# Second expert loop of a four-layer kernel: batch 0's rows gathered from slot 27 on, tile stores shared out anew, one register load per slot

## The chip, the cores and the metric

The kernel is one program on one core of a Trainium2 chip. The metric is the device time of one execution in microseconds (us); lower is better.

## The reference, cut to what matters

Four batches of 512 tokens with 128 features pass through four pairs of a cross-attention and a feed-forward block, all in fp32. Two of the feed-forward blocks are mixtures of experts:

```python
# L0: 8 experts, each token goes to one;  L1: 16 experts, each token goes to its three best
x = x + L0_ffn(layernorm(x))      # top_idx = argmax(gate_logits); y = relu(x @ w1[e] + b1[e]) @ w2[e] + b2[e]
x = x + L1_xattn(layernorm(x), ctx)
raw_gate = softmax(x_ @ gate); _, topk_idx = top_k(raw_gate, 3)
x = x + sum over e of gate_topk[..., e] * (relu(x_ @ W1[e] + b1[e]) @ W2[e] + b2[e])    # L1_ffn
x = x + L2_xattn(layernorm(x), ctx)
...
```

## The kernel before, in words

The program's steps are numbered 0 to 7 (attention 0, experts 1, attention 2, experts 3, attention 4, feed-forward 5, attention 6, feed-forward 7). Steps 1 and 3 are **expert loops**. Each engine has its own instruction stream, written out by hand and joined to the others by semaphores, so the order of the code is the order of the work.

**Routing.** For each batch VectorE finds every token's experts and its rank among the tokens of that expert (`route`). GpSimd then writes the normalised rows to their places in `rowbuf` in DRAM by indirect DMAs (`scatter`, 12 for a batch in step 3, two in flight). Every expert has a region there, so its tokens stand in order of batch, and a tile is 128 rows of one region.

**Slots.** The loop goes through the tiles in slots: 23 in step 1, 63 in step 3. In a slot SyncE (SP) loads the tile `xs` from `rowbuf` (`tile_load`), TensorE transposes it (`turn`), multiplies it by the expert's first weights one slot later (`hidden`) and by its second ones two slots later (`second`); ScalarE takes the transposed tile out and applies the bias and the relu. VectorE copies the first weights of a slot four ahead of their use and adds the last bias four slots later (`add_bias`), which writes the tile `ys`. There are 8 places for `xs` and 8 for `ys`. A tile `ys` is stored in `outbuf` by SP, 8 slots behind its load, or in step 3 by GpSimd: all odd slots up to 31 (`own_store`, `SHARE`).

**Which tile stands in which slot** is worked out on the chip, by small matmuls on TensorE and short operations on VectorE: `early_list` gives the first tiles (`EARLY`: 4 and 8) as soon as three batches are routed, and `tile_list` the rest once all four are. Each list is read into registers: SP reads a tile's place (`tiles_of`, one register load per slot, 31 slots ahead), TensorE and VectorE read its expert (`known_at`: from slot `FROM` on two numbers per slot, until all are known). After the first 8 slots of step 3, SP writes one tile of zero rows behind each of the 16 regions.

**Gathering.** GpSimd reads the rows of each batch back by indirect DMAs, 4 per batch in step 1 and 12 in step 3 (`gather`, two in flight). Before a batch it waits until the slots that can hold that batch's rows are stored: `PRIOR[l][b]` is their number, and it waits for the last 8 of them. VectorE adds the gathered rows to `x` (`add_experts`): in step 3 batch 0 beside slots 54, 56 and 58, batch 1 beside slots 59 and 61 and after the loop, batches 2 and 3 inside attention 4. GpSimd also works out the root of each batch's variance (`power`), between the gathers.

```python
PRIOR = {1: (15, 19, 19, 23), 3: (35, 47, 51, 63)}
SHARE = 33
```

## Time and profile before

| | us |
|---|---|
| median of 3 runs | 554.27 (553.14 to 560.3) |
| the profiled execution, its own time | 557.48 |
| span from its first to its last instruction | 555.8 |

| engine | busy us | share of the span |
|---|---|---|
| TensorE (PE) | 418.5 | 75% |
| VectorE (DVE) | 333.5 | 60% |
| ScalarE (ACT) | 239.4 | 43% |
| GpSimd (POOL) | 226.9 | 41% |

The rows of the profile come from that one execution, so a stage is read against its 557.48 us, of which 1.7 lie outside the span. No engine is busy all the time: what counts at each place is which wait ends last. In this execution the first expert loop takes the stretch from 77 to 136 us, attention 2 that from 136 to 210, the second loop that from 229 to 342, and attention 4 follows.

### The profile page before, as it was taken

To read this page: it belongs to the slowest core of one execution; us is meant where nothing else is said; L and a number is where in the kernel's file an instruction comes from. 1 tells how busy PE (TensorE), PEld (TensorE's weight loads), DVE (VectorE), ACT (ScalarE), POOL (GpSimd) and SP (SyncE) were. 2 spreads that over 40 slices of the span, in tenths; PEclk is the share of its full clock that TensorE was granted. 3 is DMA by queue.
4 is the path that set the end of the run, shared out by engine and by line. 5 is a ranking of instruction groups with operands and counts; after the bars stand their busy time and mean duration, and the time that the engine had idled before them with its cause. 6 is when DMAs were issued, how large, how long until landed. Compare 5 with 4: busy or idle time off the path is not lost.

```text
span 555.8 us, 10030 instructions
## 1 busy us (share of the span) xinstructions
PE 418.5 (75%) x2604; PEld 347.2 (62%) x2604; DVE 333.5 (60%) x1141; ACT 239.4 (43%) x635; POOL 226.9 (41%) x286
## 2 busy tenths in 40 slices
PE   5788758997889898549899436857799999972550
PEld 4667748897567685338799435536586768761440
DVE  5755535563878765124445317477676577858887
ACT  2333315554444422425677223433555755652321
POOL 3512740016515777641114655663311254543215
PEclk9795559998999857678999778778699999995555
DMA  7899646782191111343335322110000000000002
GB/s 194 269 404 406 158 141 214 274 296 71 36 357 47 49 38 39 110 119 106 95 103 153 94 57 60 37 44 10 0 2 1 1 0 2 1 0 1 1 1 75
DMA packets 63301, 56.50 MB, mean 102 GB/s; under 512 B 12180, under 2 KB 49262, under 8 KB 63118
## 3 DMA queue, kind: packets, MB, share of 16 engines
q1 hardware_dynamic: 56094, 44.98, 25.3%
q0 software_dynamic: 4608, 9.45, 5.8%
q10 hardware_dynamic: 2544, 1.44, 0.9%
q8 instruction: 23, 0.38, 0.3%
q14 instruction: 32, 0.26, 0.2%
HBM read 24.12 MB, written 31.72 MB: 100 GB/s over the span
## 4 chain that ended last, share of the span: by engine, by line
PE 27%; DMA 19%; DVE 17%; SPq 12%; issue 9%; POOL 7%; DVEq 5%; ACT 4%; POOLq 0%; ACTq 0%
SPq L424 12%; DMA rowbuf<-h_sb,slots 7%; PE bank L2236 5%; PE bank L2249 5%; DMA vZ<-outbuf,slots 5%; PE bank L2090 4%; POOL rowbuf L638 3%; PE bank L2106 3%; DMA h_sb<-outbuf,slots 3%; PE bank L2095 2%; PE bank L2228 2%; ACT xn L1625 2%; DVE stats L823 2%; POOL rstd L615 2%; DMA outbuf<-h_sb 1%
## 5 line engine op out<-in xcount | busy, mean ns | idle before, releaser
L2249 PE MATMUL bank<-wall,r 128*128 x436 | 70.3, 296 | 20.1 <-DVE h_sb L1292 19.8
L1719 ACT ACTIVATE r<-bank,b 128x128 f32<-128x128 f32 x218 | 66.1, 366 | 34.1 <-PE bank L2236 33.8
L615 POOL TENSOR_TENSOR rstd<-veps,mhalf 128x4 f32<-128x4 f32 x32 | 33.8, 1057 | 114.0 <-DVE veps L828 113.7
L638 POOL DMA_INDIRECT rowbuf<-h_sb,slots x64 | 62.6, 978 | 34.9 <-DMA rowbuf<-h_sb,slots 14.9
L2249 PEld LDWEIGHTS bank<-wall,r 128*128 128x128 f32 x436 | 60.1, 206 | 22.3 <-issue 21.3
L665 POOL DMA_INDIRECT vZ<-outbuf,slots x40 | 39.1, 978 | 65.0 <-DMA outbuf<-h_sb 46.2
L2236 PE MATMUL bank<-on,e_sb 128*128 128x128 f32 x348 | 58.4, 301 | 0.0
L2106 PEld LDWEIGHTS bank<-vB,eT 128*128 128x128 f32 x384 | 51.7, 209 | 0.0
L2106 PE MATMUL bank<-vB,eT 128*128 128x36 f32 x384 | 51.5, 284 | 0.0
L2236 PEld LDWEIGHTS bank<-on,e_sb 128*128 128x128 f32 x348 | 50.6, 213 | 0.0
L1711 ACT COPY on<-bank 128x128 f32<-128x128 f32 x86 | 23.1, 268 | 63.4 <-PE bank L2228 61.5
L1649 ACT COPY eT<-bank 128x512 f32<-128x512 f32 x48 | 28.1, 585 | 47.1 <-PE bank L2095 47.1
L1292 DVE TENSOR_TENSOR h_sb<-bank,b2all 128x128 f32<-128x128 f32 x86 | 24.7, 289 | 37.6 <-PE bank L2249 37.3
L1298 DVE COPY e_sb<-wall 128x256 f32 (+1 forms) x75 | 25.1, 337 | 31.8 <-PE bank L2236 19.9
L2228 PE MATMUL bank<-ident,h_sb 128*128 128x128 f32 x86 | 26.7, 311 | 22.4 <-DMA h_sb<-rowbuf 15.4
L2095 PEld LDWEIGHTS bank<-ident,e_sb 128*128 128x128 f32 x192 | 25.9, 154 | 23.2 <-issue 10.8
L2090 PE MATMUL bank<-aB,xnT_all 128*128 128x512 f32 x64 | 35.3, 640 | 5.3 <-DVE e_sb L1229 4.6
L2095 PE MATMUL bank<-ident,e_sb 128*128 128x128 f32 x192 | 32.5, 297 | 3.1 <-ACT e_sb L1645 2.0
L2228 PEld LDWEIGHTS bank<-ident,h_sb 128*128 128x128 f32 x86 | 13.1, 153 | 30.3 <-DMA h_sb<-rowbuf 17.7
L823 DVE BATCH_NORM_STATS2 stats<-x 128x6 f32<-128x128 f32 x128 | 27.9, 281 | 2.9
L1225 DVE TENSOR_REDUCE mx<-bank 128x16 f32<-128x512 f32 x32 | 21.9, 684 | 10.8 <-PE bank L2090 10.5
L1625 ACT ACTIVATE xn<-x,nmr,rstd 128x128 f32<-128x128 f32 x48 | 19.7, 483 | 15.7 <-POOL nmr L622 15.7
(303 smaller groups left out, 845.9 us busy)
## 6 DMA issues: line engine op xcount, KB each, us to landing
outbuf<-zero SPq DMA_DIRECT2D x17, 1024.0 KB, 13.6
wall<-in_w SPq DMA_DIRECT2D x4, 2048.0 KB, 13.9
h_sb<-rowbuf SPq DMA_DIRECT2D x86, 64.0 KB, 2.0
outbuf<-h_sb SPq DMA_DIRECT2D x70, 64.0 KB, 1.9
rowbuf<-zero SPq DMA_DIRECT2D x24, 64.0 KB, 1.5
x<-in_x ACTq DMA_DIRECT2D x4, 256.0 KB, 6.3
rowbuf<-h_sb,slots POOLq DMA_INDIRECT x64, 2.2
b2all<-in_L_ffn_b SPq DMA_DIRECT2D x1, 1024.0 KB, 15.1
```

Source lines behind the costliest of these rows:

```text
L424: sp.dma_start(dst, src).then_inc(s, 16)
L615: r = nc.gpsimd.tensor_tensor(rstd[:, at], veps[:, at], mhalf[:, 0:W], ALU.pow)
L638: placed = nc.gpsimd.indirect_dma_start(rowbuf[0:MOE[l][0] * REGION * P], bass.IndirectOffsetOnAxis(slots[:, k * T + t:k * T + t + 1], 0), ...
L665: nc.gpsimd.indirect_dma_start(tile_of(yg[l][b], w * K + k), None, outbuf[0:MOE[l][0] * REGION * P], bass.IndirectOffsetOnAxis(slots[:, c: ...
L823: v.bn_stats(stats[:, w * 6:w * 6 + 6], src(w))
L1719: i = a.activation(hT[:, u * 512 + c * P:u * 512 + (c + 1) * P], bank[2 + u][:, c * P:(c + 1) * P], ACT.Relu, bias=b1[l][:, bass.ds(e * C ...
L2090: mm(s_ps[t % 2][:, :], tile_of(xnT_all, t), aB[l][:, (t // W) * 512:(t // W + 1) * 512], start=True, stop=True).then_inc(s_s, 1)
L2095: i = nc.tensor.transpose(tile_of(e_ps[t % 2], c), e_sb[:, (t % 2) * 512 + c * P:(t % 2) * 512 + (c + 1) * P], ident[:, :])
L2106: i = mm(o_ps[p % 2][:, at + c * VC:at + (c + 1) * VC], eT[:, (t % 2) * 512 + c * P:(t % 2) * 512 + (c + 1) * P], vB[l][:, ((t // W) * 4 + ...
L2228: nc.tensor.transpose(bank[4 + s % 2][:, 0:P], tile_of(xs, s % PLACES), ident[:, :]).then_inc(s_xt, 1)
L2236: h = mm(tile_of(bank[2 + s % 2], c), tile_of(w1s[l][s % RING], c), tile_of(xsT, s % 2), start=True, stop=True)
L2249: y = mm(bank[6 + s % 2][:, 0:P], hT[:, (s % 2) * 512 + c * P:(s % 2) * 512 + (c + 1) * P], wall[:, bass.ds(e * n + (WHALF + c * P), P)], ...
```

## The change

- **`early_list`** sorted its tiles by expert alone: those that are whole after three batches. Now tiles that are whole after batch 0 come first, then those whole after batch 1, then those whole after batch 2 (`WHOLE = 3`). Their number stays 4 and 8. It takes wider operations and some more matmuls.
- **`PRIOR`** follows from that: batch 0's rows are bound to the first 11 slots of step 1 (15 before) and the first 27 of step 3 (35 before), batch 1's to the first 15 of step 1 (19 before) and the first 39 of step 3 (47 before). Those of batches 2 and 3 stay.
- **`SHARE`**: GpSimd stores slots 11, 13, 15, 17, 19 and 21, six tiles instead of sixteen. SP stores all others.
- **`known_at`**: TensorE and VectorE load one expert number per slot from slot `FROM` on, up to slot 21 of step 1 and slot 58 of step 3, where they loaded two per slot up to slots 12 and 31.
- **Order on GpSimd** behind the second loop: three gathers of batch 2 stand ahead of `power(16)`, five between it and `power(17)`, four behind that; of batch 3 five stand ahead of `power(18)` and seven behind.
- On VectorE one masked copy (`cap6`) moves from slot 6 to slot 12. The constant tables `span_to` are laid out anew and get smaller.

```diff
-PRIOR = {1: (15, 19, 19, 23), 3: (35, 47, 51, 63)}
-SHARE = 33
+PRIOR = {1: (11, 15, 19, 23), 3: (27, 39, 51, 63)}
+SHARE = range(11, 23, 2)
...
         def own_store(s):
-            return s % 2 and s < SHARE
+            return s in SHARE
...
         def known_at(l, s):
-            first = EARLY[l] + 2 * (s - FROM[l])
-            return range(first, min(SLOT_TILES[l], first + 2)) if s >= FROM[l] else ()
+            k = EARLY[l] + s - FROM[l]
+            return (k,) if EARLY[l] <= k < SLOT_TILES[l] else ()
...
-            gather(3, 1, 1)
+            gather(3, 1)
+            gather(3, 2, 0, 3)
             power(16)
-            gather(3, 2, 0)
+            gather(3, 2, 3, 8)
             power(17)
-            gather(3, 2, 1)
-            gather(3, 3, 0)
+            gather(3, 2, 8)
+            gather(3, 3, 0, 5)
             power(18)
-            gather(3, 3, 1)
+            gather(3, 3, 5)
...
@@ early_list on VectorE, stage 0 @@
-                    v.tensor_scalar(rounded[0:E, 0:M], at[0:E, 0:M], -63.5, ROUND, ALU.add, ALU.add)
+                    v.tensor_scalar(rounded[0:E, 0:n], at[0:E, 0:n], -63.5, ROUND, ALU.add, ALU.add)
                     dve.drain()
-                    v.tensor_scalar(lens[0:E, 0:M], rounded[0:E, 0:M], ROUND, None, ALU.subtract).then_inc(s_ln, 1)
+                    v.tensor_scalar(filled[0:E, first + EARLY[3]:first + EARLY[3] + n], rounded[0:E, 0:n], ROUND, None, ALU.subtract)
+                    dve.drain()
+                    v.tensor_tensor(lens[0:E, 0:n], filled[0:E, first + EARLY[3]:first + EARLY[3] + n],
+                                    filled[0:E, first + EARLY[3] - M:first + EARLY[3] - M + n], ALU.subtract).then_inc(s_ln, 1)
...
@@ early_list on TensorE, stages 1 and 2 @@
-                    mm(at[0:M, 64:64 + 3 * E], lens[0:E, 0:M], span_to[l][0:E, first:first + 3 * E], start=False, stop=True, skip_group_check=True).then_inc(s_le, 1)
+                    for k in range(WHOLE):
+                        i = mm(at[0:M, 64:64 + 2 * Q].rearrange("p (i q) -> p i q", i=2), lens[0:E, k * M:(k + 1) * M],
...
-                    mm(at[0:E, 320:320 + NS], one_seg[0:M, 0:E], ones[0:M, 0:NS], start=True, stop=True).then_inc(s_lr, 1)
+                    for k in range(WHOLE):
+                        i = mm(at[0:E, 320:320 + NS], one_seg[0:M, k * E:(k + 1) * E], ones[0:M, 0:NS], start=(k == 0), stop=(k == WHOLE - 1))
```

GpSimd at the end of the second loop, before. The DMA to `outbuf` is the last tile store, those that read `outbuf` are gathers (of batch 0 into `h_sb`, of batches 1 and 2 into `vZ`, of batch 3 into `wall`), and the three operations on `rstd` and `nmr` are one `power`:

```order
L652 DMA outbuf<-h_sb 128x128
L665 DMA h_sb<-outbuf,slots 128x128 x12
L665 DMA vZ<-outbuf,slots 128x128 x12
L615 TENSOR_TENSOR rstd<-veps,mhalf 128x4
L620 TENSOR_SCALAR nmr<-mv 128x4
L622 TENSOR_TENSOR nmr<-nmr,rstd 128x4
L665 DMA vZ<-outbuf,slots 128x128 x6
L615 TENSOR_TENSOR rstd<-veps,mhalf 128x4
L620 TENSOR_SCALAR nmr<-mv 128x4
L622 TENSOR_TENSOR nmr<-nmr,rstd 128x4
L665 DMA vZ<-outbuf,slots 128x128 x6
```

and with the change:

```order
L659 DMA outbuf<-h_sb 128x128
L672 DMA h_sb<-outbuf,slots 128x128 x12
L672 DMA vZ<-outbuf,slots 128x128 x15
L622 TENSOR_TENSOR rstd<-veps,mhalf 128x4
L627 TENSOR_SCALAR nmr<-mv 128x4
L629 TENSOR_TENSOR nmr<-nmr,rstd 128x4
L672 DMA vZ<-outbuf,slots 128x128 x5
L622 TENSOR_TENSOR rstd<-veps,mhalf 128x4
L627 TENSOR_SCALAR nmr<-mv 128x4
L629 TENSOR_TENSOR nmr<-nmr,rstd 128x4
L672 DMA vZ<-outbuf,slots 128x128 x4
L672 DMA wall<-outbuf,slots 128x128 x5
```

Three of batch 2's gathers have moved ahead of the first `power`, and the ones behind it are dealt out 5 and 4 instead of 6 and 6.

SP in the second loop at slots 8 and following, before; TENSOR_LOAD is the register load of a tile's place, the DMA from `rowbuf` loads a tile and that to `outbuf` stores one:

```order
L543 DMA outbuf<-h_sb 128x128
L527 TENSOR_LOAD at_list
L540 ISA
L540 DMA h_sb<-rowbuf 128x128
L527 TENSOR_LOAD at_list
L540 ISA
L540 DMA h_sb<-rowbuf 128x128
L543 DMA outbuf<-h_sb 128x128
```

and with the change:

```order
L549 DMA outbuf<-h_sb 128x128
L533 TENSOR_LOAD at_list
L546 ISA
L546 DMA h_sb<-rowbuf 128x128
L549 DMA outbuf<-h_sb 128x128
L533 TENSOR_LOAD at_list
L546 ISA
L546 DMA h_sb<-rowbuf 128x128
```

Every load is followed by a store now, where every second one was.

TensorE in the second loop, before; TENSOR_LOAD reads expert numbers, the product with `ident` is `turn`, that with `on` is `hidden`, those with `wall` are `second`:

```order
L2240 TENSOR_LOAD es_late x2
L2228 MATMUL bank<-ident,h_sb 128x128
L2236 MATMUL bank<-on,e_sb 128x128 x2
L2249 ISA
L2249 MATMUL bank<-wall,r 128x128
L2249 ISA
L2249 MATMUL bank<-wall,r 128x128
```

and with the change:

```order
L2254 TENSOR_LOAD es_late
L2242 MATMUL bank<-ident,h_sb 128x128
L2250 MATMUL bank<-on,e_sb 128x128 x2
L2263 ISA
L2263 MATMUL bank<-wall,r 128x128
L2263 ISA
L2263 MATMUL bank<-wall,r 128x128
```

One register load stands ahead of each slot's transpose in place of two.

## Rows read from the trace of the kernel before

**Rows 1.** The chain that ended last, in order of time: start us, us, what
```profile
245.93 2.04 DMA h_sb<-rowbuf
...
288.93 3.77 DMA outbuf<-h_sb
...
293.62 1.02 POOL h_sb L665
```

**Rows 2.** Timeline of VectorE (in brackets: idle time before it, and its releaser)
```profile
279.25 0.29 DVE L1292 TENSOR_TENSOR h_sb<-bank,b2all 128x128 f32<-128x128 f32 x1
...
314.22 1.14 DVE L1279 SCALAR_TENSOR_TENSOR x<-h_sb,gk,x 128x128 f32<-128x128 f32 x4 [7.77 <-DMA h_sb<-outbuf,slots]
...
332.40 1.14 DVE L1279 SCALAR_TENSOR_TENSOR x<-vZ,gk,x 128x128 f32<-128x128 f32 x4 [10.56 <-DMA vZ<-outbuf,slots]
...
359.10 2.35 DVE L1279 SCALAR_TENSOR_TENSOR x<-vZ,gk,x 128x128 f32<-128x128 f32 x8 [4.13 <-DMA vZ<-outbuf,slots]
```

**Rows 3.** Timeline of GpSimd beside and behind the second expert loop
```profile
311.56 0.94 POOL L665 DMA_INDIRECT h_sb<-outbuf,slots  x1 [0.57 <-DMA h_sb<-outbuf,slots]
313.36 0.94 POOL L665 DMA_INDIRECT vZ<-outbuf,slots  x1 [0.86 <-DMA h_sb<-outbuf,slots]
...
329.84 0.94 POOL L665 DMA_INDIRECT vZ<-outbuf,slots  x1 [0.63 <-DMA vZ<-outbuf,slots]
335.69 1.09 POOL L615 TENSOR_TENSOR rstd<-veps,mhalf 128x4 f32<-128x4 f32 x1 [4.91 <-DVE veps L828]
...
346.64 1.06 POOL L615 TENSOR_TENSOR rstd<-veps,mhalf 128x4 f32<-128x4 f32 x1
...
356.53 0.94 POOL L665 DMA_INDIRECT vZ<-outbuf,slots  x1 [0.61 <-DMA vZ<-outbuf,slots]
```

**Rows 4.** Timeline of SyncE's queue in the second expert loop, early and late
```profile
251.09 0.38 SPq L543 DMA_DIRECT2D outbuf<-h_sb  x1
251.96 1.16 SPq L540 DMA_DIRECT2D h_sb<-rowbuf  x2
253.22 0.38 SPq L543 DMA_DIRECT2D outbuf<-h_sb  x1
...
301.13 0.33 SPq L540 DMA_DIRECT2D h_sb<-rowbuf  x1
...
302.13 0.33 SPq L540 DMA_DIRECT2D h_sb<-rowbuf  x1
```

**Rows 5.** Timeline of TensorE: transposes of slots 29 to 32, and a wait behind the loop
```profile
279.12 0.30 PE L2228 MATMUL bank<-ident,h_sb 128*128 128x128 f32 x1
...
280.55 0.30 PE L2228 MATMUL bank<-ident,h_sb 128*128 128x128 f32 x1 [0.17 <-issue]
...
281.64 0.28 PE L2228 MATMUL bank<-ident,h_sb 128*128 128x128 f32 x1
...
282.81 0.27 PE L2228 MATMUL bank<-ident,h_sb 128*128 128x128 f32 x1
...
363.63 1.12 PE L2090 MATMUL bank<-VW,xnT_all 128*128 128x512 f32 x2 [1.68 <-DVE e_sb L1229]
```

**Rows 6.** Timeline of all engines at the end of the first expert loop
```profile
122.22 1.01 POOL L665 DMA_INDIRECT vZ<-outbuf,slots  x1 [44.41 <-DMA outbuf<-h_sb]
...
129.59 0.94 POOL L665 DMA_INDIRECT vZ<-outbuf,slots  x1 [0.81 <-issue]
...
130.38 0.69 DVE L1272 TENSOR_TENSOR x<-x,vZ 128x512 f32<-128x512 f32 x1 [3.65 <-DMA vZ<-outbuf,slots]
...
133.33 3.17 PE L2249 MATMUL bank<-wall,r 128*128 x16 [2.42 <-DVE h_sb L1292]
```

**Rows 7.** Timeline of all engines from the early list to batch 3's scatters
```profile
204.44 0.37 PE L2035 MATMUL bank<-ones,one_seg 8*16 8x63 f32 x2
...
215.91 0.17 DVE L1049 CAST slots<-slot_f 128x12 int32<-128x12 f32 x1
...
218.38 1.08 POOL L638 DMA_INDIRECT rowbuf<-h_sb,slots  x1 [0.54 <-issue]
```

More of the change, by code:

```diff
@@ L52 @@
 FROM = {1: 3, 3: 4}
+WHOLE = 3
+LISTED = {1: (1, 2), 3: (1, 2)}
+TURNED = {1: 0, 3: 0}
 LAG = 4
@@ L359, in stored, with own_stores @@
             if l == 3 and own_store(s):
-                return s_yp[u], 16 * len(range(u, s + 1, PLACES))
-            shared = len(range(u, SHARE, PLACES)) if l == 3 and u % 2 else 0
-            return s_ys[u], 16 * (placed_by(l, u, s + 1) - shared)
+                return s_yp[u], 16 * own_stores(u, s)
+            return s_ys[u], 16 * (placed_by(l, u, s + 1) - (own_stores(u, s) if l == 3 else 0))
+        def own_stores(u, s):
+            return sum(own_store(k) for k in range(u, s + 1, PLACES))
         def placed_by(l, u, s):
@@ L562, in _ @@
                         sp.wait_ge(s_es, list_no(l) + 2)
+                        at = {k: at[k] for k in at if k >= s - PLACES}
                         at.update(tiles_of(l, s, min(SLOT_TILES[l], s + AHEAD + 1)))
@@ L652, in tile_store, with gather @@
                 nc.gpsimd.dma_start(outbuf[bass.ds(values[0] * P, P)], tile_of(ys, s % PLACES)).then_inc(s_yp[s % PLACES], 16)
-            def gather(l, b, part):
+            def gather(l, b, first=0, last=None):
                 K = TOPK[l]
-                if part == 0:
+                if first == 0:
                     for s in range(PRIOR[l][b] - PLACES, PRIOR[l][b]):
                         pool.wait_ge(*stored(l, s))
-                for w in (2 * part, 2 * part + 1):
-                    for k in range(K):
-                        c = k * T + b * W + w
-                        i = GATHERS[l] + (b * W + w) * K + k
-                        last_but_one_landed(i)
-                        nc.gpsimd.indirect_dma_start(tile_of(yg[l][b], w * K + k), None, outbuf[0:MOE[l][0] * REGION * P], bass.IndirectOffsetOnAxis(slots[:, c:c + 1], 0)).then_inc(s_rows[i % 2], 16)
+                for n in range(first, W * K if last is None else last):
+                    w, k = n // K, n % K
+                    c = k * T + b * W + w
+                    i = GATHERS[l] + b * W * K + n
+                    last_but_one_landed(i)
+                    nc.gpsimd.indirect_dma_start(tile_of(yg[l][b], w * K + k), None, outbuf[0:MOE[l][0] * REGION * P], bass.IndirectOffsetOnAxis(slots[:, c:c + 1], 0)).then_inc(s_rows[i % 2], 16)
             def add_bo(b):
```

78 lines of the change are left out of this document (38 added, 40 removed).

## The prediction

> **What bounds the kernel now.** I read the chain of waits in order of time first, since no engine is busy all along. From the first load of slot 8 on [rows 1] the reader is to see TensorE working slot after slot, until the store of slot 34 at 288.93; from there the chain leaves the loop and goes over GpSimd's gathers, of which the first starts at 293.62, when that store has landed [rows 1]. Then I read GpSimd's timeline: batch 0's twelve gathers run from 293.62 to 311.56, batch 1's from 313.36 to 329.84, batch 2's last one starts at 356.53 [rows 3]. They wait for nothing but each other (two in flight) and for the `power` operations between them. Last comes VectorE's timeline, which shows who pays: it stands 7.77 us ahead of batch 0's sum, 10.56 ahead of batch 1's and 4.13 ahead of batch 2's [rows 2]. So TensorE's speed in the slots beyond 34 is worth nothing; the chain is the start of batch 0's gathers plus the number and the spacing of gathers behind it. The first loop has the same pattern in small: batch 0's first gather starts at 122.22 and VectorE waits 3.65 for the four of them [rows 6].
>
> **Term 1, the start of batch 0's gathers.** It waits for slot 26 in place of slot 34. Before, slot 26's `ys` was ready at 279.25 [rows 2], 9.7 ahead of slot 34's store. Two edits move that point again.
>
> TensorE: two register loads per slot stand ahead of the transpose up to slot 30. The transposes of slots 29 and 30 are 1.43 apart; those of 30 and 31, with one load between, 1.09; those of 31 and 32, with none, 1.17 [rows 5]. So a pair costs about 0.3 and a single one is hidden behind the 1.1 of matmul work. Over the some 15 slots from 11 (earlier ones are slowed by other things) to 26 that is up to 4.3, and slot 26 would be ready at 274.9. If each load cost half of the pair, it would be 277.1. The loads that now stand in slots 32 to 58 cost, by the same two prices, nothing or 0.15 each, 4.1 in all, which the 10.56 that VectorE waits at slot 59 [rows 2] covers.
>
> SP: it now stores the odd slots 1 to 9 and 23 to 31 too. Before, two loads, two register loads and one store took 2.13 (store at 251.09 to store at 253.22). The second load stands 0.83 behind the first (251.96 + 1.16 - 0.33 = 252.79), the store 0.43 behind that, and the next load 0.87 behind a store [rows 4]. Late in the loop, where no register load is left, a load and a store take 1.00 [rows 4], so the step from a store to a load is 0.57. That makes 0.30 for a register load, 1.30 for an iteration with everything, and 0.83 for one without the store. From 245.93 [rows 1] SP goes through iterations 8 to 18 (11 of 1.30), 19 to 29 (6 of 0.83, 5 of 1.30), 30 and 31 (1.30) and 32 and 33 (1.00): 30.4 us. It loads slot 34 at 276.4 and stores slot 26 at 276.8. That is later than TensorE by the low price (274.9) and level with it by the high one, so 276.8 holds in both cases. A store from GpSimd is no longer among them beyond slot 21.
>
> What the Trainium skill says in "DMA: Bandwidth & Descriptors", section "Issuing engines are not separate DMA queues", is that issuing from several engines saves only the issue time of the sequencer. By that rule the edit costs what SP's rows show and nothing beyond.
>
> With 2.0 to land, as the load at 245.93 took, and 0.9 until the gather starts [rows 1], the first gather comes at 279.7 in place of 293.62: **13.9 earlier**. The store of slot 34 took 3.77 to land [rows 1]; if slot 26's does too, it is 12.0. An iteration of SP might cost the whole 2.13 of a pair instead; that end is a rival below.
>
> **Term 2, the spacing.** Beside the running loop eleven steps took 17.9 (1.63 each), batch 1's, most of them with the loop standing, 16.5 (1.50 each) [rows 1, 3]. VectorE stood at slot 54 at 306.4 (314.22 - 7.77) [rows 2]; it comes there some 4 earlier, has five slots of 1.1 and parts of two sums to go, and reaches slot 59 at about 308, so batch 0's twelve and some five of batch 1's run beside the loop: 5 x 0.13 = **0.7 later**; at most all of batch 1's, 1.4. Batch 1's gate, slot 38, is stored some twelve slots after slot 26 and thus about 13 us later, well inside batch 0's 19; batch 2's gate, slot 50, falls near 303, before batch 1 is done. The moved gates thus stay covered.
>
> **Term 3, between batch 1 and batch 2.** Batch 1's last gather starts at 329.84, and `power` for batch 0 at 335.69, after 4.91 of idling, because VectorE's statistics stand behind the sum of batch 1 [rows 3]. Three gathers of 1.5 fill this hole. `power` stays where it is against 329.84; five gathers follow instead of six, so the next `power` (346.64 before) comes 1.6 earlier, and batch 2 is complete 5.3 earlier. But TensorE works in order: it gets the next transposed batch only 1.6 earlier, and had 1.68 of idling before it met VectorE again at 363.63 [rows 5]. So it lets through 3.3 and the gathers 5.3; I take **3.7 earlier**, near the smaller, since TensorE and VectorE then have to meet at each step. Batch 3's order costs nothing: its five gathers ahead of `power` fit, since the statistics come some 10 us after batch 2's last gather.
>
> **Term 4, the first loop.** Batch 0's gate goes from slot 14 to slot 10. Four slots are at least 4.4 even at the second loop's 1.1 per slot, so its four gathers are over before VectorE comes to slot 22, and the 3.65 go [rows 6]. TensorE idled 2.42 of them, and its 3.17 for the sixteen passes that follow hold some more of that waiting [rows 6]. Between 2.4 and 3.65 I take **3.1 earlier**. Batch 1's gate goes from slot 18 to slot 14, whose store had landed when the gather at 122.22 began [rows 6]; so batch 1's four are over ahead of 129.59, where they started before, and its sum, which comes only when attention 2 has begun, finds them there. The gain lasts through attention 2 into the scatters, which start when batch 0 is routed and run without a break up to 245.93.
>
> **Costs at nothing.** The longer `early_list` has six more small matmuls and two more VectorE operations in step 3, at most 0.37 us each by the longest of before [rows 7], 2.2 together for the matmuls. They delay the routing of batch 3: its places are ready at 215.91 and first used at 218.38 [rows 7], a cover of some 2.3, of which little is left; without it the whole loop would start up to 2.2 later. In step 1 the same work lies ahead of the wait for the biases of the experts. The masked copy goes from the slots ahead of the pause before 245.93 to slot 12, where VectorE has two operations like the 0.29 of [rows 2] in a slot of 1.1 to 1.4; uncovered it would cost its own length once, under 1. The tables cost nothing.
>
> **The sum.** 13.9 - 0.7 + 3.7 + 3.1 = 20.0. The profiled execution took 557.48, so it would take 537.5. It lies 3.2 above the median of the runs, so against that I forecast 554.27 - 20.0 = **534.3 us**, 3.6% less. With the late end of every term (12.0 - 1.4 + 3.3 + 2.4 = 16.3) it is 538.0, with the early end (13.9 + 5.3 + 3.65 = 22.9) 531.4.
>
> **Rivals.**
> *GpSimd is held up by VectorE.* The gathers now run beside weight copies of VectorE, one per slot. For: they are 0.13 farther apart beside the loop. Against: a gather occupies GpSimd for 0.94 both at 311.56, beside it, and at 329.84, without it [rows 3]. If each of the 17 gathers beside the loop waited for one VectorE instruction of 0.29 [rows 2], it would be 4.9 more: 539.2. "SBUF — State Buffer", section "SBUF: two separate sides", in the Trainium skill has the rule that GpSimd cannot write its descriptors while VectorE runs an fp32 copy within SBUF; the trace, with 0.94 in both places, doesn't show it.
>
> *Only the middle is kept.* Terms 3 and 4 are given back, one because attention 4 has TensorE working nearly without a gap, the other because attention 2 behind it is paced by VectorE. For: each is limited by another engine that I could follow for some steps only. Then 13.9 - 0.7 = 13.2 are left: 541.1.
>
> *SP becomes the bound, and the kernel slower.* SP's iterations 8 to 34 take as long as the pair of before, 2.13, because stores rather than loads were what took SP's time. Then slot 26 is stored near 301.7 and the gathers start at 304.6, 11.0 later than now; with 0.7 for the spacing and 6.8 still gained elsewhere it is 4.9 slower: 559.2. It decides from about 1.9 per iteration. Against: late in the loop SP does a load and a store in 1.00 [rows 4].
>
> *The change doesn't do what it says,* if something other than the store of slot 34 held the gathers back. But 293.62 follows its landing (288.93 + 3.77 = 292.70) by 0.92 [rows 1]. I leave it in the last case's chance.
>
> **How the numbers follow.** The forecast has 0.70, held-up gathers 0.12, only the middle 0.13, slower 0.05. A difference under 2% (11.1 us, 543.2) is about what a measurement of this kernel can't tell from no change. The first three cases lie beyond it by their middle; from the third some 0.08 fall short of it, and a little of the second. That makes 0.88 faster, 0.08 the same, 0.04 slower. The range that leaves out 2 in 10 reaches from 529.5 (the early end, and some us for the spread of the runs) to 541.5 (the third case).
>
> **What would show it.** In the profile after, the first gather into `h_sb` about 17 us earlier than 293.62 (13.9, and 3.1 from the first loop); SP's loads and stores in turn, 1.3 apart; transposes 1.1 to 1.25 apart from slot 12 on; no wait of VectorE ahead of batch 0's sum in either loop, but still some 10 ahead of batch 1's in the second; three gathers into `vZ` in GpSimd's idle 4.91; batch 2's sum within 26 us of batch 1's last gather. Wrong would be the forecast if SP's iterations took over 1.6, if the gathers were 2 apart, or if batch 3's scatters waited for its places.

## The result, and the profile after

The changed kernel takes 539.21 us (median of 4 runs, 535.93 to 544.56), the kernel before beside it 554.18 (4 runs, 553.14 to 560.3): a ratio of 0.970, 95% interval 0.961 to 0.979. That is 15.0 us less by the medians. The profiled execution took 540.01 us against 557.48, 17.5 less, and its span is 538.3 against 555.8. The mean granted TensorE clock is 0.827 against 0.820. Here and below medians are of all executions and ratios of the fast ones alone (544.56 is a slow one), and the profiles of experiments 8, 9 and 10 are of slow executions.

The chain that ended last, in order of time, of the kernel after (start us, us, what), from the first load of slot 8 to the first gather, with the piece around the store of slot 26:

```profile
243.72 1.77 DMA h_sb<-rowbuf
...
272.81 0.30 DVE h_sb L1298
273.11 0.34 SPq L549
273.46 0.04 issue
273.50 0.27 SPq L533
...
276.98 0.34 SPq L546
277.32 0.04 issue
277.36 0.04 SPq L549
277.40 0.34 issue
277.73 2.08 DMA outbuf<-h_sb
...
279.96 0.77 issue
280.73 2.63 DMA h_sb<-outbuf,slots
```

The gathers now follow the store of slot 26 at 277.73, where before they followed that of slot 34 at 288.93 [rows 1]; the first comes 12.9 earlier. But the last pieces ahead of it are no longer TensorE's: they are SyncE issuing one store, one register load (L533, 0.27) and one tile load after another. VectorE's last operation on slot 26's `ys` starts at 273.99 and takes 0.29, so the tile lay ready for 3.4 us before its store at 277.73, as VectorE's timeline of the kernel after shows (the row of L1298; in before it was 279.25 [rows 2]):

```profile
124.95 0.69 DVE L1278 TENSOR_TENSOR x<-x,vZ 128x512 f32<-128x512 f32 x1 [0.16 <-DMA vZ<-outbuf,slots]
...
273.99 0.29 DVE L1298 TENSOR_TENSOR h_sb<-bank,b2all 128x128 f32<-128x128 f32 x1
...
303.67 1.14 DVE L1285 SCALAR_TENSOR_TENSOR x<-h_sb,gk,x 128x128 f32<-128x128 f32 x4 [0.17 <-DMA vZ<-outbuf,slots]
...
321.28 1.14 DVE L1285 SCALAR_TENSOR_TENSOR x<-vZ,gk,x 128x128 f32<-128x128 f32 x4 [10.09 <-DMA vZ<-outbuf,slots]
...
343.60 1.56 DVE L1285 SCALAR_TENSOR_TENSOR x<-vZ,gk,x 128x128 f32<-128x128 f32 x5 [0.16 <-issue]
```

(The first line is batch 0's sum in the first loop.) Of VectorE's four waits in before [rows 2, 6] three are gone: 3.65 ahead of batch 0's sum in the first loop, 7.77 ahead of it in the second, 4.13 ahead of batch 2's. The one ahead of batch 1's stays (10.09 after 10.56).

GpSimd's timeline of the kernel after, the rows that answer to [rows 3]:

```profile
280.73 1.03 POOL L672 DMA_INDIRECT h_sb<-outbuf,slots  x1 [11.25 <-DMA outbuf<-h_sb]
...
298.25 0.94 POOL L672 DMA_INDIRECT h_sb<-outbuf,slots  x1 [0.30 <-DMA outbuf<-h_sb]
301.44 0.95 POOL L672 DMA_INDIRECT vZ<-outbuf,slots  x1 [2.24 <-DMA h_sb<-outbuf,slots]
...
318.65 0.95 POOL L672 DMA_INDIRECT vZ<-outbuf,slots  x1 [0.43 <-DMA vZ<-outbuf,slots]
...
324.57 1.09 POOL L622 TENSOR_TENSOR rstd<-veps,mhalf 128x4 f32<-128x4 f32 x1 [0.21 <-DVE veps L830]
...
334.03 1.05 POOL L622 TENSOR_TENSOR rstd<-veps,mhalf 128x4 f32<-128x4 f32 x1 [0.46 <-DVE veps L830]
...
340.23 0.95 POOL L672 DMA_INDIRECT vZ<-outbuf,slots  x1 [0.69 <-DMA vZ<-outbuf,slots]
```

Three gathers fill what was an idle time of 4.91 ahead of batch 0's step; 0.21 is left. Read against before, the profiled difference of 17.5 us comes in five pieces:

| piece, read between | before | after | gain | forecast |
|---|---|---|---|---|
| first loop and attention 2: load of slot 8 | 245.93 | 243.72 | 2.2 | 3.1 |
| load of slot 8 to first gather | 47.7 | 37.0 | 10.7 | 13.9 |
| first gather to last of batch 1 | 36.2 | 37.9 | -1.7 | -0.7 |
| last of batch 1 to batch 2's sum | 29.3 | 25.0 | 4.3 | 3.7 |
| batch 2's sum to the end of the span | 196.7 | 194.7 | 2.0 | 0 |

### The profile page after: what moved, and what is told of

Its sections match the earlier page's. It is cut to its first block, busy times and chain, and to the rows that moved or that the text cites. A ratio compares the mean times of both kernels' runs of the same rounds, so it can differ in the third digit from the quotient of the medians.

```text
span 538.3 us, 10062 instructions
## 1 busy us (share of the span) xinstructions
PE 415.3 (77%) x2628; PEld 344.9 (64%) x2628; DVE 336.5 (63%) x1143; ACT 240.1 (45%) x635; POOL 221.6 (41%) x276
## 4 chain that ended last, share of the span: by engine, by line
PE 30%; DMA 18%; DVE 18%; POOL 13%; issue 10%; ACT 5%; DVEq 4%; SPq 1%; POOLq 0%; ACTq 0%
POOL rowbuf L645 8%; DMA vZ<-outbuf,slots 5%; PE bank L2104 4%; DMA rowbuf<-h_sb,slots 4%; PE bank L2250 4%; PE bank L2263 4%; DMA h_sb<-outbuf,slots 3%; PE bank L2120 3%; PE bank L2109 2%; POOL rstd L622 2%; PE bank L1959 2%; DMA wall<-outbuf,slots 2%; ACT xn L1631 2%; DVE stats L825 1%; DVE x L1285 1%
## 5 line engine op out<-in xcount | busy, mean ns | idle before, releaser
L1725 ACT ACTIVATE r<-bank,b 128x128 f32<-128x128 f32 x218 | 66.3, 366 | 36.1 <-PE bank L2250 35.3
L2263 PE MATMUL bank<-wall,r 128*128 x436 | 69.5, 293 | 11.9 <-DVE h_sb L1298 10.9
L645 POOL DMA_INDIRECT rowbuf<-h_sb,slots x64 | 63.0, 985 | 34.0 <-DMA rowbuf<-h_sb,slots 15.5
L1298 DVE TENSOR_TENSOR h_sb<-bank,b2all 128x128 f32<-128x128 f32 x86 | 24.8, 290 | 38.0 <-PE bank L2263 36.4
L2242 PE MATMUL bank<-ident,h_sb 128*128 128x128 f32 x86 | 26.9, 313 | 18.4 <-DMA h_sb<-rowbuf 16.5
L2104 PE MATMUL bank<-aB,xnT_all 128*128 128x512 f32 x64 | 37.0, 667 | 3.8 <-DVE e_sb L1235 3.0
```

Source lines behind the costliest of these rows:

```text
L645: placed = nc.gpsimd.indirect_dma_start(rowbuf[0:MOE[l][0] * REGION * P], bass.IndirectOffsetOnAxis(slots[:, k * T + t:k * T + t + 1], 0), ...
L1725: i = a.activation(hT[:, u * 512 + c * P:u * 512 + (c + 1) * P], bank[2 + u][:, c * P:(c + 1) * P], ACT.Relu, bias=b1[l][:, bass.ds(e * C ...
L2104: mm(s_ps[t % 2][:, :], tile_of(xnT_all, t), aB[l][:, (t // W) * 512:(t // W + 1) * 512], start=True, stop=True).then_inc(s_s, 1)
L2242: nc.tensor.transpose(bank[4 + s % 2][:, 0:P], tile_of(xs, s % PLACES), ident[:, :]).then_inc(s_xt, 1)
L2263: y = mm(bank[6 + s % 2][:, 0:P], hT[:, (s % 2) * 512 + c * P:(s % 2) * 512 + (c + 1) * P], wall[:, bass.ds(e * n + (WHALF + c * P), P)], ...
```

## Experiments

Twelve runs of nine kernels were made in three groups, each group on one chip with the kernel before beside it. On the first group's chip before had a median of 556.72 us, on that of the other two 569.96 and 570.07; what that second chip does differently is told with the fifth run. So places are compared by their distance from the load of slot 8, and sizes in the time by the difference of two ratios, times 555 us. By the intervals of the ratios such a difference is uncertain by about 6 us to either side, so the places in the traces carry the argument and the times only go along with it.

**1. The second loop's gates put back.**

```diff
-PRIOR = {1: (11, 15, 19, 23), 3: (27, 39, 51, 63)}
+PRIOR = {1: (11, 15, 19, 23), 3: (35, 47, 51, 63)}
```

> The changed kernel with the second loop's gates put back to 35 and 47 slots (the lists and all else stay new). Theory A (the moved gate gives most of the gain): the first gather into h_sb starts 8 slots later, some 9 to 10 us behind its place in the changed kernel measured from the load of slot 8 (37.0 us there, so 46 to 47 here), the time rises by 8 to 10 us to 547 to 549. Rival B (the gain comes from the order on GpSimd and the first loop, and the loop catches the gathers up again): under 3 us are lost, 540 to 542.

Measured: 547.44 us (546.87 to 548.35, 4 runs), ratio to before 0.982, interval 0.977 to 0.988. The first gather comes 45.5 us behind the load of slot 8 (37.0 in after), batch 1's last one 36.1 behind that (37.9). GpSimd's timeline shows what it waited for:

```profile
267.30 0.54 POOL L659 DMA_DIRECT2D outbuf<-h_sb  x1 [1.82 <-DVE h_sb L1298]
287.37 1.03 POOL L672 DMA_INDIRECT h_sb<-outbuf,slots  x1 [19.53 <-DMA outbuf<-h_sb]
```

So the gates are 8.5 at the start and, since the gathers stand closer when more of them run behind the loop, 6.7 at batch 1's last. Theory A holds, with the first gather 0.5 earlier than it said. In the time it is 6.9 (0.982 less 0.970), nearly half of the gain; the two intervals just touch (0.977 and 0.979).

**2. SyncE relieved.** GpSimd stores the odd slots 1 to 25 in place of 11 to 21.

```diff
-SHARE = range(11, 23, 2)
+SHARE = range(1, 27, 2)
```

> The changed kernel with GpSimd storing the odd slots 1 to 25 (13 tiles) in place of 11 to 21. Theory A (SP's queue, not TensorE, holds slot 26's store, 3.7 us behind its ys): SP's load of slot 34 and the store of 26 come 2.5 to 3.5 us earlier, the gathers start 33.5 to 34.5 us after the load of slot 8 in place of 37.0, and the time falls by 2 to 3.5 us to 536 to 537. Rival B (TensorE's 1.2 us per slot sets the pace, SP only follows): the gathers start less than 1 us earlier and the time stays within 1 us. Rival C (stores by GpSimd land later or hold its queue): slower by 1 us or more.

Measured: 537.49 us (534.44 to 541.82, 6 runs), ratio 0.965, interval 0.960 to 0.971. The first gather comes 32.2 us behind the load of slot 8, 4.8 less than in after:

```profile
270.39 0.54 POOL L659 DMA_DIRECT2D outbuf<-h_sb  x1 [1.93 <-DVE h_sb L1298]
274.49 1.02 POOL L672 DMA_INDIRECT h_sb<-outbuf,slots  x1 [3.55 <-DMA outbuf<-h_sb]
```

TensorE's transpose of slot 26 came 24.6 behind the load of slot 8 (26.2 in after), 1.6 earlier, which can't give the 4.8; SyncE's load of slot 34 came 29.3 behind it (33.3 in after), 4.0 earlier. Seven stores of 1.33 - 0.83 (an iteration of SyncE with and without one) are 3.5 of that. At batch 2's last gather the lead over after is 3.9 (92.6 us behind the load of slot 8, in place of 96.5). SyncE thus was the bound between slot 8 and slot 26: theory A, by more than its 2.5 to 3.5. The ratio is the lowest of all, 2.7 us under after's, but its interval overlaps that of after: the trace shows the gain, the times don't separate the two kernels.

**3. Two register loads per slot until all are known, as before.**

```diff
-            k = EARLY[l] + s - FROM[l]
-            return (k,) if EARLY[l] <= k < SLOT_TILES[l] else ()
+            first = EARLY[l] + 2 * (s - FROM[l])
+            return range(first, min(SLOT_TILES[l], first + 2)) if s >= FROM[l] else ()
```

> The changed kernel with two register loads per slot on TensorE and VectorE until all are known, as before the change. Theory A (a pair costs 0.3 us per slot up to slot 31, a single one 0.1): transposes of slots 12 to 30 are 1.4 apart in place of 1.2, slots from 32 on 1.1 in place of 1.2; ys of slot 26 comes 3 us later, close to where SP stores it now, so the gathers start 0 to 1.5 us later and the time rises by 0 to 1.5 us (539 to 541). Rival B (the single loads give a large part of the gain): 3 us or more slower, 542 and above.

Measured: 538.74 us (537.49 to 542.47, 4 runs), ratio 0.969, interval 0.963 to 0.976. First gather 35.9 behind the load of slot 8, batch 1's last 35.6 behind the first. In the time the edit shows nothing, which is what theory A allows. In the trace it shows at three places. In the first loop TensorE goes from the transpose of slot 4 to that of slot 12 in 20.4 us here and in 20.0 in before (86.84 to 106.81), but in 18.1 in after and in 17.1 to 17.2 in experiments 1, 2 and 4. TensorE's timeline here and then in after:

```profile
85.39 0.33 PE L2242 MATMUL bank<-ident,h_sb 128*128 128x128 f32 x1
...
105.78 0.27 PE L2242 MATMUL bank<-ident,h_sb 128*128 128x128 f32 x1
```

```profile
85.37 0.33 PE L2242 MATMUL bank<-ident,h_sb 128*128 128x128 f32 x1 [0.52 <-DMA h_sb<-rowbuf]
...
103.50 0.30 PE L2242 MATMUL bank<-ident,h_sb 128*128 128x128 f32 x1 [0.30 <-issue]
```

In the second loop the pairs make slot 26's `ys` 2.1 later (32.4 behind the load of slot 8, 30.3 in after), as theory A has it, but SyncE comes to its store only at 32.9 (34.0 in after), so they don't hold the gathers up. Behind slot 34, where only after still has loads, twenty slots take 24.0 us with them and 21.8 without, which the gathers cover.

**4. The old order of GpSimd behind the loop.**

```diff
-            gather(3, 2, 0, 3)
             power(16)
-            gather(3, 2, 3, 8)
+            gather(3, 2, 0, 6)
             power(17)
-            gather(3, 2, 8)
-            gather(3, 3, 0, 5)
+            gather(3, 2, 6)
+            gather(3, 3, 0, 6)
```

> The changed kernel with GpSimd's old order behind the loop: power(16) ahead of batch 2's gathers, 6 and 6 of each batch around the other powers. Theory A: GpSimd idles some 4 to 5 us again ahead of power(16), batch 2's sum comes 29 us after batch 1's last gather in place of 25, and the time rises by 3.5 to 4.5 us to 543 to 544. Rival B (attention 4 is bound by TensorE, the order hides): under 1.5 us slower.

Measured: 542.34 us (540.92 to 544.17, 4 runs), ratio 0.974, interval 0.968 to 0.980. GpSimd's timeline has the idle time back:

```profile
321.91 1.08 POOL L622 TENSOR_TENSOR rstd<-veps,mhalf 128x4 f32<-128x4 f32 x1 [4.92 <-DVE veps L829]
...
332.64 1.07 POOL L622 TENSOR_TENSOR rstd<-veps,mhalf 128x4 f32<-128x4 f32 x1
```

From batch 1's last gather to batch 2's last it is 25.6 us (21.6 in after, 26.7 in before), and VectorE waits 3.47 ahead of batch 2's sum. So the order is worth 4.0 there, as theory A has it. In the time it is 2.3, less than theory A said, and the intervals overlap: the trace shows the gain, the times don't.

**5. The first loop's gates put back.**

```diff
-PRIOR = {1: (11, 15, 19, 23), 3: (27, 39, 51, 63)}
+PRIOR = {1: (15, 19, 19, 23), 3: (27, 39, 51, 63)}
```

> The kernel after, with the first loop's gates put back to (15, 19, 19, 23). Theory A (the gates of the first loop carry the whole gain in that stage, the profile after has loop 2's load of slot 8 2.2 us earlier than before): VectorE's wait before batch 0's sum in the first loop comes back at 2.5 to 3.7 us, the load of slot 8 in the second loop comes at 245.5 to 246.5, and the time is about 541 us (539.2 plus 2.2). Theory B (the first loop's gain is from the other edits there, the single register loads and the moved list): no wait comes back, and the time stays within 0.7 us of the kernel after.

Measured: 557.02 us (553.02 to 562.15, 4 runs) where before took 569.96; ratio 0.985, interval 0.975 to 0.995. The wait of VectorE is back, as theory A has it:

```profile
127.80 0.69 DVE L1278 TENSOR_TENSOR x<-x,vZ 128x512 f32<-128x512 f32 x1 [2.53 <-DMA vZ<-outbuf,slots]
```

but the first scatter starts at 167.44, no later than after's 168.77, and the load of slot 8 at 244.5 and not at 245.5 to 246.5. Nor does attention 2 start as late as with the first loop of before. TensorE's timeline has its first transposes here at

```profile
132.93 0.60 PE L2092 MATMUL bank<-ident,x 128*128 128x128 f32 x4
```

and in experiment 6, on the same chip and with before's first loop, at

```profile
136.73 1.06 PE L2080 MATMUL bank<-ident,x 128*128 128x128 f32 x4
```

(137.37 in experiment 7). So both theories hold in part: the wait hangs on the gate, and 3.8 to 4.4 us of the earlier start of attention 2 come without it, from the other edits in the first loop; experiment 3 shows the single register loads as one of them. (Experiments 8 and 9, with the early gate but with the pairs of loads, start attention 2 at 133.82 and 136.51.) The last part of this section says where some of the gain goes.

The time of this run tells little, because the second chip does something that the first doesn't. Windows of this kernel there (us, busy of PE, PEld, DVE, ACT, POOL, granted clock, DMA share, GB/s):

```profile
270.00:280.00 10.00, 10.00 (x78) 9.37 (x78) 4.96 (x17) 7.11 (x26) 0.06 (x1) 1.00 0.40 113
280.00:290.00 10.00, 7.90 (x48) 7.08 (x48) 2.85 (x10) 4.36 (x16) 5.76 (x7) 0.84 0.50 134
...
310.00:320.00 10.00, 5.80 (x25) 5.22 (x25) 1.76 (x6) 2.66 (x10) 3.77 (x4) 0.50 0.24 67
320.00:330.00 10.00, 9.91 (x74) 9.10 (x74) 5.80 (x22) 6.52 (x23) 1.92 (x2) 0.95 0.35 100
```

Gathers run from 279.94 to 314.47. Up to the first of them TensorE does 78 passes in 10 us, beside them 25 to 48, and behind them 74 again. From slot 34 to slot 54 it takes 45.6 us in place of after's 24.0. All eight profiles from that chip show it (slots 34 to 54 take 34 to 46 us there; the first chip's take 22 to 24), and it begins a few us behind the first gather wherever that stands. The instructions of VectorE and ScalarE don't get longer beside the gathers (the bias 0.29, the relu 0.36, as ahead of them); what grows are the waits between the engines, up to 3.54 us ahead of a bias, and TensorE's passes at the lower clock. The same chip also takes 77 to 87 us from the first scatter to the load of slot 8, where all profiles of the first take 74.6 to 74.9 and after 75.0. So there the loop beside early gathers is slow; batch 1's or batch 2's gate becomes the bound, and VectorE's wait ahead of batch 1's sum shrinks to 0.21.

**6, 7. Before, with the new order alone.** The edit is that of experiment 4 in the other direction, made in the kernel before.

```diff
+            gather(3, 2, 0, range(0, 3))
             power(16)
-            gather(3, 2, 0)
+            gather(3, 2, 0, range(3, 8))
             power(17)
-            gather(3, 2, 1)
-            gather(3, 3, 0)
+            gather(3, 2, 1, range(8, 12))
+            gather(3, 3, 0, range(0, 5))
```

> The kernel before, with only GpSimd's new order of gathers and normalisation steps behind the second loop (three gathers of batch 2 ahead of batch 0's step, five of batch 3 ahead of the step of batch 2). Nothing else is changed. Theory A (in before GpSimd's idle 4.91 us ahead of batch 0's step and the split of batch 2's twelve gathers are what the order saves, and this does not need the earlier gates): batch 1's last gather to batch 2's last takes 22 us in place of 26.7, batch 2's sum comes 4 us earlier than 359.10, and the time is 2.5 to 4 us below before's. Theory B (without the earlier gates the three gathers of batch 2 wait on slots up to 50 and only delay batch 0's step): the gain is under 1 us.

> The same kernel as before_new_order (before with only GpSimd's new order behind the second loop), run again since in that run's profile every engine but GpSimd was stretched from 280 to 325 us. Theory A (the order alone saves the waits of 4.91 and 4.13 us of before): batch 1's last gather to batch 2's last takes 22 us, batch 2's sum comes about 4 us earlier than 359.10, and the time is 2.5 to 4 us below before's (ratio 0.993 to 0.995). Theory B: under 1 us (ratio over 0.998).

Measured: 564.5 us (554.35 to 567.33, 12 runs), ratio 0.986, interval 0.974 to 0.998, and in the second try 565.93 (560.93 to 571.77, 12 runs), ratio 0.997, interval 0.992 to 1.001. The place does what theory A says: from batch 1's last gather to batch 2's last 21.1 and 21.6 us (26.7 in before), and no idle time ahead of batch 0's step. But batch 1's gathers now wait for their gate (profile of the second try):

```profile
321.18 0.94 POOL L666 DMA_INDIRECT h_sb<-outbuf,slots  x1 [0.42 <-DMA h_sb<-outbuf,slots]
331.75 0.94 POOL L666 DMA_INDIRECT vZ<-outbuf,slots  x1 [9.63 <-DMA outbuf<-h_sb]
...
354.22 1.04 POOL L615 TENSOR_TENSOR rstd<-veps,mhalf 128x4 f32<-128x4 f32 x1
```

This is the slowed loop again. Both intervals allow 0.992 to 0.998, which is 1 to 4 us; more than that they don't say. So the trace bears theory A out, and the time leaves both open.

**8, 9. The gates without the shorter list of GpSimd's stores.** Stores at slots 1, 3 to 31, two register loads per slot, the old order (those two edits are the ones of experiments 3 and 4); the gates and the early list stay.

```diff
-SHARE = range(11, 23, 2)
+SHARE = range(1, 33, 2)
```

> The kernel after, with everything of the second loop but the gates put back: GpSimd stores slots 1, 3 to 31 as before, register loads come in twos, the order behind the loop is the old one; the gates (11, 15, 19, 23) and (27, 39, 51, 63) and the early list stay. Theory A (GpSimd reaches its gathers only behind its last store, and that store is slot 31's, so the early gate is worth little without the shorter list of stores): the first gather comes at 284 to 288 and the time is 546 to 551 us. Rival B (the gate alone carries it, the stores of slots 27 to 31 are ready soon enough): the first gather comes at 276 to 281, and the time is 540 to 543 us.

> The same kernel as gates_alone (the kernel after with GpSimd's stores at 1, 3 to 31, loads in twos and the old order), run again for the same reason. Theory A (the early gate is worth little while GpSimd has stores up to slot 31 ahead of its gathers): first gather 39 to 42 us behind the load of slot 8, in place of 37.0 in after and 47.7 in before, and the time 5 to 9 us under before's. Rival B (the gate alone carries it): 36 to 37 us, and 12 to 14 us under before's.

Measured: 566.49 us (556.93 to 569.83, 10 runs), ratio 0.989, interval 0.982 to 0.996; in the second try 571.67 (558.64 to 573.25, 4 runs) where before had 570.07, which gives no usable ratio. The first gather comes 39.6 and 41.5 us behind the load of slot 8. GpSimd's timeline (first try) shows why:

```profile
296.68 0.54 POOL L659 DMA_DIRECT2D outbuf<-h_sb  x1 [1.64 <-DVE h_sb L1297]
297.73 1.03 POOL L672 DMA_INDIRECT h_sb<-outbuf,slots  x1 [0.52 <-issue]
```

The store of slot 31 stands right ahead of it in GpSimd's queue. The gate alone gives 6.2 to 8.1 of the 10.7, and then GpSimd's own last store is the bound, as theory A has it; the second expectation's 39 to 42 was met. The absolute numbers of the first one (284 to 288, and 546 to 551 us) were missed, since the load of slot 8 comes at 258.15 in that profile, 14.4 later than in after; 10.9 of that arise between the first scatter and this load.

**10, 11. VectorE's sum of batch 1 moved behind the loop,** on top of the stores of experiment 2.

```diff
-LATE = (0, 4, 8)
+LATE = (1, 4, 8)
...
-                    if l == 3 and s in (NS - 4, NS - 2):
-                        add_experts(3, 1, ((s + 4 - NS) // 2,))
...
+                if l == 4 and t == 0:
+                    add_experts(3, 1)
+                    stats_of(norm_no(4, 1), 1)
...
-            gather(3, 1)
-            gather(3, 2, 0, 3)
+            gather(3, 1, 0, 10)
             power(16)
-            gather(3, 2, 3, 8)
+            gather(3, 1, 10)
+            gather(3, 2, 0, 5)
             power(17)
```

> The kernel after with GpSimd's stores at slots 1, 3 to 25 (which gave 537.5 us), and VectorE's sum of batch 1 moved from slots 59 to 63 of the second loop to the first tile of the attention, with batch 1's normalisation and transposes one tile later and two of its gathers behind batch 0's step. In the kernel after VectorE waits 9 to 10 us for batch 1's gathers inside the loop, and TensorE's last slots wait with it. Theory A (the chain of gathers on GpSimd sets the end, VectorE's wait is slack that the attention would spend anyway): the last slots end some 9 us earlier, but batch 2's sum moves by under 2 us, and the time is 535.5 to 538 us. Theory B (the wait on the path costs in full, because the attention of batch 0 starts late): the attention's first tiles come 5 us or more earlier and stay so, and the time is 530 to 533 us.

> The same kernel as late_sums (stores of GpSimd at slots 1, 3 to 25, and VectorE's sum of batch 1 moved behind the loop), run again for the same reason. The earlier run gave a ratio of 0.991 where the kernel with those stores alone had 0.965 on another chip. Theory A (the chain of gathers sets the end, and the move of the sum is worth nothing): ratio 0.963 to 0.969. Theory B (the wait inside the loop is on the path): 0.955 or less. Theory C (the move costs, because two of batch 1's gathers and batch 2's come behind the normalisation step and the attention of batch 1 then waits): over 0.972.

Measured: 563.15 us (558.43 to 571.02, 12 runs), ratio 0.991, interval 0.987 to 0.995, and 565.26 (559.23 to 570.52, 12 runs), ratio 0.997, interval 0.991 to 1.002. The first expectation had no case for this; the second, written after that result, has it as theory C. GpSimd's timeline (second try):

```profile
332.29 1.09 POOL L622 TENSOR_TENSOR rstd<-veps,mhalf 128x4 f32<-128x4 f32 x1 [19.12 <-DVE veps L830]
...
335.44 0.95 POOL L672 DMA_INDIRECT vZ<-outbuf,slots  x1 [0.30 <-issue]
```

I had put two of batch 1's gathers behind batch 0's step, and that step needs the statistics that VectorE makes at slot 60. With the loop slowed GpSimd stood 19.12 us there with gathers still to issue. The first gather came 32.4 us behind the load of slot 8 in both, as in experiment 2, so all of the loss lies behind it. Experiment 12 is the kernel to compare with, since it ran beside the second try and differs from it by this edit and two stores: its ratio is 0.9815, some 8 us less, and from its first gather to batch 2's last it takes 67.5 us in place of 82.2. So the move costs, as theory C has it, with the chip the same for both. Whether the sum inside the loop costs anything is not settled: the same edit moved the gathers.

**12. GpSimd's stores at the odd slots 1 to 21.**

```diff
-SHARE = range(11, 23, 2)
+SHARE = range(1, 23, 2)
```

> The kernel after with GpSimd's stores at the odd slots 1 to 21, so SyncE keeps slots 23 and 25. With stores up to slot 25 (537.5 us on the earlier chip, ratio 0.965) the first gather waited 3.55 us behind GpSimd's last store for the last stores to land, so GpSimd was not late. Theory A (what counts is that SyncE has fewer than two transfers for each slot while it catches up, not which engine stores the last slots before the gate): the first gather comes 31 to 33 us behind the load of slot 8, as with stores up to 25, and the ratio is 0.963 to 0.967. Theory B (SyncE is just caught up at slot 23 and the two slots more put it behind): 34 to 36 us, and a ratio of 0.967 to 0.971.

Measured: 557.14 us (552.54 to 565.2, 6 runs), ratio 0.9815, interval 0.973 to 0.991; both expectations for the ratio were missed; I put that down to what the second chip does to the loop. The first gather comes 33.1 us behind the load of slot 8, just beyond theory A's 31 to 33 and 3.9 under after's: it is the early odd slots, while SyncE catches up, that count, and slots 23 and 25 account for 0.7 to 0.9 (the first gather came at 32.4 with them on this chip, at 32.2 on the other).

**What became of the first loop's gain.** Attention 2's first transposes start at 131.39 after 136.29, 4.9 earlier, more than the whole wait of 3.65, since the slots ahead got faster too (experiments 3 and 5). The first scatter starts at 168.77 after 171.22, 2.4 earlier. Windows of TensorE and the others behind the first loop, of the kernel before and then of the kernel after (columns as above):

```profile
146.00:156.00 10.00, 8.72 (x60) 6.65 (x58) 8.59 (x28) 4.80 (x8) 4.77 (x5) 1.00 0.45 136
```

```profile
141.00:151.00 10.00, 10.00 (x39) 7.72 (x38) 6.78 (x21) 3.62 (x7) 3.40 (x4) 0.51 0.48 145
151.00:161.00 10.00, 10.00 (x74) 8.20 (x73) 7.08 (x23) 5.21 (x9) 1.97 (x2) 1.00 1.08 401
```

The same stretch of attention 2, 10 to 20 us behind its start, ran at a granted clock of 1.00 (2.4 GHz) in before and at 0.51 (1.2 GHz) in after, with 39 passes in place of 60. In the 10 us ahead of it TensorE was busy 6.67 of 10 in both. From the first transposes to the first scatter it takes 34.9 us in before and 37.4 in after. The other profiles go the same way. Experiments 1 to 4 have 0.52 to 0.75 from 10 to 20 us behind their start of attention 2 and take 37.3 to 37.4. On the second chip experiments 5, 11 and 12 have 1.00 there and in the 10 us on either side and take 34.4 to 34.6; experiments 8 (0.51) and 10 (0.66 in the next 10 us) take 38.5 and 37.4, and 6, 7 and 9, with 0.70 or 0.84 in another stretch, 35.9 to 36.1. So 2.5 of the 4.9 are lost to the lower clock. What makes the clock fall in one profile and not in the other I did not find; that it stays up in before and falls in after and all four kernels of the first group may be no accident, but no run shows what it hangs on.

## Why the prediction was right, and where it was off

The forecast was 534.3 us in a range of 529.5 to 541.5; 539.21 lies in it, by the mechanism that the forecast names. It was too early by 4.9. Half of that is inside the profiled executions (20.0 forecast, 17.5 measured); the other half is that the two profiled executions differ by 2.5 more than the medians do. Within the 17.5 there is some luck: the four terms gave 15.5, and 2.0 came at the end, where nothing was forecast.

**What bounds the kernel** was read rightly. With the second loop's gates late, 8.5 of the gain at the first gather go (experiment 1); what TensorE does beyond slot 34 took no part that shows: its slots there are 1.2 apart in after and 1.1 in before and in experiment 3, and the times of after and experiment 3 are the same.

**Term 1** was mis-sized: 10.7 in place of 13.9. The step that failed is SyncE's count of 30.4 us up to the load of slot 34. Its timeline in the kernel after:

```profile
250.78 0.35 SPq L546 DMA_DIRECT2D h_sb<-rowbuf  x1
...
252.09 0.35 SPq L546 DMA_DIRECT2D h_sb<-rowbuf  x1
...
256.51 1.62 SPq L549 DMA_DIRECT2D outbuf<-h_sb  x1
258.63 0.35 SPq L546 DMA_DIRECT2D h_sb<-rowbuf  x1
...
272.26 1.19 SPq L549 DMA_DIRECT2D outbuf<-h_sb  x1
```

An iteration with everything and no held issue took 1.31 to 1.36, as worked out (1.30). What the count had no place for are issues that are held: 1.62 in place of 0.38 at 256.51, 1.19 at 272.26, 0.67 at 267.73, 0.4 in an early iteration. With some 0.03 more in each full iteration, and 0.30 less in that of slot 31, which has no register load any more, that makes about the 33.3 from the load of slot 8 to that of slot 34; and the store comes 0.75 behind it and not 0.43. The held issues are no accident of this execution: experiments 1, 3, 4 and 5, with the same code on SyncE, have one too 13 to 14 us behind the load of slot 8 (0.76 to 1.59) and another one 27 to 29 us behind it (0.68 to 1.27). Before has one in the same stretch as well (two loads from 263.50 on take 2.33 together, where such a pair takes 1.16 [rows 4]), so its trace could have told. The chain names VectorE's biases at 256.86 and 272.81 as the releasers, but these are of later slots than the stores are, so what held them stays open. The landing of 2.08 and the 0.92 to the gather were right (2.0 and 0.9). That SyncE and not TensorE would set the point was said; experiments 2 and 3 show it. TensorE even waited for a load of SyncE's, as its timeline shows at slot 29; its transposes at slots 33 to 35 are 1.1 to 1.2 apart:

```profile
274.25 0.33 PE L2242 MATMUL bank<-ident,h_sb 128*128 128x128 f32 x1 [0.47 <-DMA h_sb<-rowbuf]
...
279.02 0.30 PE L2242 MATMUL bank<-ident,h_sb 128*128 128x128 f32 x1
280.11 0.27 PE L2242 MATMUL bank<-ident,h_sb 128*128 128x128 f32 x1
281.35 0.30 PE L2242 MATMUL bank<-ident,h_sb 128*128 128x128 f32 x1
```

The price of a register load on SyncE, 0.30, is confirmed by the chain's L533 of 0.27. The rule cited from the Trainium skill, "DMA: Bandwidth & Descriptors", section "Issuing engines are not separate DMA queues", by which another issuing engine saves only the sequencer's issue time, fits experiment 2: of its 4.8 us, 3.5 are SyncE's queue time for seven stores.

**Term 2** was 1.7 and not 0.7, above the bound of 1.4. Batch 0's eleven steps took 17.5 (17.9 before), batch 1's 17.2 (16.5 before), together 0.3 more. The rest is the step from batch 0's last to batch 1's first, 3.2 in place of 1.8: the gather at 297.00 took 3.65 to land, and with two in flight the next but one waits for it. I had summed within the batches and not across them. The slow landing comes again: the step is 4.0 in experiment 2 and 3.6 in experiment 4. In experiment 3 it is 1.7, and the whole 35.6 is less than before's; what makes the difference stays open.

**Term 3** was 4.3 and not 3.7: the full 5.3 didn't pass, as argued, and experiment 4 puts the order at 4.0. It lasted up to the end of the span, where another 2.0 came. These can't be put down to the change: from batch 2's last gather to the end it is 199.3 us in before at a granted clock of 0.80 and 198.1 in after at 0.82, but 201.9 in both experiments 1 and 2, whose code there is that of after, at 0.79.

**Term 4** was 2.2 and not 3.1, and only in part by the reasoning given. The wait went with the gate, as forecast, and comes back without it (2.53 in experiment 5). But the wait was not the bound of the gain: attention 2 starts 4.9 earlier, since TensorE goes through slots 4 to 12 in 18.1 us in place of 20.0. The term left out the single register loads, though they stand in the first loop too. In experiments 6 and 7, with before's first loop, attention 2 starts 3.8 to 4.4 later than in experiment 5, which has the late gate but all the other edits. Then the clock took 2.5 back. That 2.2 is near 3.1 is luck.

**Costs at nothing**: from the first scatter to the load of slot 8 it is 74.7 us before and 75.0 after, and 74.6 to 74.9 in the first group, so the early list costs nothing that shows.

**Rivals.** Gathers held up by VectorE's copies: no; a gather takes 0.94 to 1.07 of GpSimd beside the loop (0.97 on average for the fifteen that overlap a weight copy of VectorE, 0.94 for the other nine of batches 0 and 1), and the spacing is 1.59 within batch 0. "SBUF — State Buffer", section "SBUF: two separate sides", in the Trainium skill would have them wait for each copy, which takes VectorE some 0.3; no run here shows it. Only the middle kept: no, 6.5 of the 6.8 in terms 3 and 4 came. SyncE as the bound and the kernel slower: the mechanism half came true, SyncE is the bound, but at 1.3 an iteration and not at the 1.9 from which it decides.

## What to carry to other kernels

When a gate opens early, follow the queue of the engine that has to deliver the last item for it, and of the engine that waits at it: here SyncE's backlog took 3 to 5 us, and GpSimd's own stores would have taken another 2.6 to 4.5. When an edit is made in two loops, work it out in both: the single register loads were priced in the second, where they gave nothing, and not in the first, where TensorE got faster by them. Work for an in-order engine is placed by what is ready at that moment: three gathers in the idle time of 4.91 gave 4 us, two gathers behind a step whose input was late made a wait of 19. Measure such a change on more than one chip, since how far two streams of work disturb each other was different on the two seen here.

## What the runs showed of the hardware that was not expected

- On one of two chips the loop was slow beside the gathers: slots that are 1.1 to 1.2 us apart were up to 4.3 apart (VectorE's biases at 308.09, 312.43 and 316.75 in experiment 5), at a granted clock down to 0.50. VectorE's and ScalarE's instructions kept their length (0.29 and 0.36) and the gathers their spacing of 1.4 to 1.6 us; the waits between the engines grew. Scatters took longer there too (77 to 87 us up to the load of slot 8, in place of 75). On the other chip twenty slots beside gathers took 1.09 each (experiment 3), as in before. The cause is open. I take it as the reason why the ratios of the runs there (0.98 to 1.00) don't compare with those of the first chip (0.965 to 0.982).
- The granted clock 10 to 20 us behind the start of attention 2 was 1.00 or 0.51 in kernels that did the same work there. From that start to the first scatter it took 34.4 to 34.9 us in the profiles at full clock and 37.3 to 38.5 in those with 0.51 to 0.75 there or just behind.
- An issue on SyncE's queue that takes 0.33 to 0.38 was held for 0.7 to 1.6 in all, at nearly the same two places behind the load of slot 8 in all five kernels with the same code on SyncE, with no wait that the profile explains.
